# The last tile of softmax rows transposed by TensorE instead of by DVE's 32x32 turns and a DMA exchange

## What is computed

```
q    = x @ Wq.T + bq
p    = softmax(q @ keys.T / sqrt(128))          # keys: 4096 x 128
x1   = layernorm(x + (p @ values) @ Wo.T + bo)
h    = silu(x1 @ W1.T * s1) * (x1 @ W2.T * s2)
h    = gelu(h @ H1.T * s_h1);  h = gelu(h @ H2.T * s_h2)
out  = layernorm(x1 + h @ W3.T * s3)
```

## Time and profile before

| | |
|---|---|
| Time, median of 3 runs | 1117.41 us (1116.58 to 1117.55) |
| Time of the profiled execution | 1117.46 us |
| Its span, first to last instruction | 1115.5 us |
| PE, DVE, ACT, POOL busy | 97%, 87%, 81%, 58% of the span |
| Frames end (last scores moved) | about 725 us |
| PE starts the first hidden layer of block 0 | 760.3 us |

### The profile page before, as it was taken

How to read it: one execution, slowest core, us unless ns; L and a number is a source line. 1 busy time by engine, 2 the same in 40 slices (tenths; PEclk the granted TensorE clock), 3 DMA queues, 4 the chain that set the end, 5 groups by cost and what they waited for, 6 DMA issues and landing times.

```text
span 1115.5 us, 20017 instructions
## 1 busy us (share of the span) xinstructions
PE 1079.3 (97%) x5324; PEld 770.6 (69%) x5324; DVE 972.2 (87%) x1806; ACT 903.1 (81%) x1609; POOL 643.0 (58%) x617
## 2 busy tenths in 40 slices
PE   6899999999999999999999999979999999999996
PEld 5666666666666666666666666646888888888875
DVE  6999999999999999999999899897888887888884
ACT  6787788878887888888878878788788888888883
POOL 0487888888888888888888888760211211121111
PEclk9999999999999999999999999999999999999998
DMA  6879888988988889888888998891010010011000
GB/s 202 203 185 212 198 201 210 209 200 202 209 203 206 203 207 210 200 202 209 206 203 204 212 200 188 193 255 55 12 46 28 28 56 28 28 35 50 11 13 27
DMA packets 83957, 165.89 MB, mean 149 GB/s; under 512 B 19664, under 2 KB 47824, under 8 KB 83792
## 3 DMA queue, kind: packets, MB, share of 16 engines
q1 hardware_dynamic: 71536, 154.29, 58.7%
q10 hardware_dynamic: 12384, 11.16, 3.5%
HBM read 22.76 MB, written 8.39 MB: 28 GB/s over the span
## 4 chain that ended last, share of the span: by engine, by line
PE 42%; SPq 13%; issue 11%; POOL 10%; ACT 10%; DMA 6%; DVE 5%; ACTq 1%; POOLq 0%; DVEq 0%
PE ring L1090 13%; SPq L380 12%; PE ring L1091 12%; POOL pT L549 10%; DMA slot_p<-rows 6%; ACT rows L629 5%; ACT pT L638 4%; PE o_ps L1017 2%; PE s_ps L1045 2%; PE s_ps L1043 2%; PE s_ps L1044 2%; PE o_ps L1020 2%; PE o_ps L1022 2%; DVE rows L795 2%; DVE rows L828 1%
## 5 line engine op out<-in xcount | busy, mean ns | idle before, releaser
L549 POOL TENSOR_TENSOR pT<-slot_p,pT 128x512 f16<-128x512 f32 x482 | 546.0, 1167 | 124.4 <-ACT pT L638 124.3
L638 ACT ACTIVATE pT<-slot_p 128x512 f16<-128x512 f32 x512 | 296.5, 617 | 73.8 <-DMA slot_p<-rows 68.6
L828 DVE TENSOR_SCALAR_CACHE_REDUCE rows<-s_ps 128x1024 f32<-128x1024 f32 x256 | 309.4, 1209 | 40.5 <-DMA slot_p<-rows 19.9
L795 DVE STREAM_TRANSPOSE rows<-rows 128x1024 f32<-128x1024 f32 x256 | 316.9, 1239 | 5.9 <-issue 4.1
L629 ACT ACTIVATE rows<-rows,bias 128x1024 f32<-128x1024 f32 x256 | 291.6, 1139 | 6.4 <-DVE bias L836 5.9
L1043 PE MATMUL s_ps<-keys,q_buf 128*128 128x512 f32 x512 | 249.2, 487 | 6.8 <-DVE rows L828 3.5
L1017 PE MATMUL o_ps<-pT,v_hi 128*128 128x512 f16 x512 | 197.4, 385 | 13.3 <-POOL pT L549 6.6
L1045 PE MATMUL s_ps<-keys,q_buf 128*128 128x512 f32 x512 | 202.4, 395 | 0.0
L1044 PE MATMUL s_ps<-keys,q_buf 128*128 128x512 f32 x512 | 201.1, 393 | 0.0
L1020 PE MATMUL o_ps<-pT,v_lo 128*128 128x256 f16 x1024 | 196.1, 273 | 0.0
L1022 PE MATMUL o_ps<-pT,v_hi 128*128 128x512 f16 x512 | 194.6, 380 | 0.0
(11 more groups left out here) (110 smaller groups left out, 1329.2 us busy)
## 6 DMA issues: line engine op xcount, KB each, us to landing
slot_p<-rows SPq DMA_DIRECT2D x1024, 128.0 KB, 3.0
x_in<-in_x SPq DMA_DIRECT2D x16, 256.0 KB, 3.4
x_in<-in_xT ACTq DMA_DIRECT2D x30, 128.0 KB, 3.3
out<-y_out SPq DMA_DIRECT2D x15, 256.0 KB, 2.4
o_scratch<-o_sum ACTq DMA_DIRECT2D x29, 128.0 KB, 2.7
o_in<-o_scratch SPq DMA_DIRECT2D x14, 256.0 KB, 3.1
z<-in_w_all ACTq DMA_DIRECT2D x25, 113.0 KB, 2.7
rows<-in_w_all SPq DMA_DIRECT2D x1, 2816.0 KB, 12.1
```

The lines of the kernel that those rows point to most:

```text
L549: nc.gpsimd.tensor_tensor(halves(s % RING, 1), slots_first(pp, s), halves(s % RING, 0), ALU.subtract).then_inc(split, 1)
L638: nc.scalar.activation(halves(s % RING, 0), slots_first(pp, s), ACT.Copy).then_inc(highed, 1)
L795: nc.vector.transpose(row_piece(tile, k), row_piece(tile, k)).then_inc(turned, 1)
L828: nc.vector.tensor_scalar(row_piece(tile, k), s_ps[:, j % 2, :], 1.0, None, ALU.mult, ALU.max, accum_out=part_max[:, tile, k:k + 1]).then_ ...
```

## The change

The second tile of the last pair is no longer turned by DVE and exchanged by DMA. Its score columns are produced in another order, by reading the keys in a pattern of 4x4x32 (`by_chunk`), so that 128 neighbouring columns of `rows` are one chunk of the values. PE then transposes 128x128 squares of fp32 from `rows` into two PSUM banks, `y_ps` and `x1_ps`, four squares at a time: a unit. ACT and DVE read the turned half of a unit from PSUM, and ACT and POOL make the parts of the first tile from `slot_p`. A unit is two value steps. In pair 30 the low parts 7, 8, 9, 11, 13 and 15 are now DVE's. `x1` of block 0 is copied by ACT after high part 10 instead of 6, and split by DVE after low part 9. The moments and the normalisation of block 1 move into the loop over units, and the transpose of its x1 goes behind V15. The raw weights are loaded in two parts; the low parts of the weights are no longer made (with this input they are not needed in either version). The four exponentials of the last tile stay behind the third and fourth high part, now with an output copy ahead of them.

```
-LATE_STEP = 12
+LOW_BY_DVE = (7, 8, 9, 11, 13, 15)
+LOW_BY_POOL = tuple(s for s in range(STEPS) if s not in LOW_BY_DVE)
+UNITS = STEPS // 2
...
+    def unit_part(u, tile, low):
+        return pT[:, 2 * u % RING:2 * u % RING + 2, :, (2 * low + tile) * P:(2 * low + tile + 1) * P].rearrange(
+            "p s c (a t) -> p (s c) a t", t=G)
+    def unit_slots(u):
+        return slot_p[:, 1, 0:GROUPS, 4 * u:4 * u + 4, :].rearrange("p a c t -> p c a t")
+    def unit_bank(u):
+        return stage.y_ps[:, :, :] if u % 2 == 0 else stage.x1_ps[:, :].rearrange("p (s d) -> p s d", d=P)
...
# SP
         exchange(PAIRS - 1, 1, 0, PIECES - 1)
-        for k in range(PIECES):
-            exchange(PAIRS - 1, 1, 1, k)
...
# POOL
+        for s in LOW_BY_POOL[STEPS - T_LAG:]:
+            low_part(PAIRS - 2, 0, s)
+        for u in range(UNITS):
+            pool.wait_ge(highed, 16 * (PAIRS - 1) + 2 * u + 1)
+            nc.gpsimd.tensor_tensor(unit_part(u, 0, 1), unit_slots(u), unit_part(u, 0, 0), ALU.subtract).then_inc(split, 1)
+            if u == 2:
                 stage.inverse_deviation(pool, 1, 0)
...
# ACT
+        def unit_high(u):
+            if u == 0:
+                for k in range(PIECES):
+                    act.wait_ge(sent[0][k], 16 * GROUPS * PAIRS)
+            act.wait_ge(pv_done, 16 * (PAIRS - 1) + 2 * u + 2 - RING)
+            nc.scalar.activation(unit_part(u, 0, 0), unit_slots(u), ACT.Copy).then_inc(highed, 1)
+            act.wait_ge(unit_made, u + 1)
+            nc.scalar.activation(unit_part(u, 1, 0), unit_turned(u), ACT.Copy).then_inc(highed, 1)
+        after_high = {3: range(PIECES)}
+        for s in range(STEPS - T_LAG, STEPS):
             high_part(PAIRS - 2, 0, s)
+            if s == 3:
+                stage.output_half(act, PAIRS - 3, 1)
+            if s in after_high:
+                for k in after_high[s]:
+                    exp_piece(PAIRS - 1, 1, k)
+            if s == 10:
                 act.wait_ge(sent[0][0], 16 * GROUPS * PAIRS)
                 stage.keep_x1T(act, 0)
...
# DVE
-        stage.residual(dve, 1)
-        for k in range(PIECES):
-            turn_piece(PAIRS - 1, 1, k)
+        stage.residual_sum(dve, 1)
         stage.output_sum(dve, PAIRS - 3, 1)
-        stage.split_x1(dve, 0)
-        for s in range(LATE_STEP, STEPS):
+        for s in LOW_BY_DVE:
             low_part(PAIRS - 2, 0, s)
+            if s == 9:
+                stage.split_x1(dve, 0)
...
+        for u in range(UNITS):
+            dve.wait_ge(highed, 16 * (PAIRS - 1) + 2 * u + 2)
+            nc.vector.tensor_tensor(unit_part(u, 1, 1), unit_turned(u), unit_part(u, 1, 0), ALU.subtract).then_inc(split_last, 1)
...
# PE
+                    if is_step(f, PAIRS - 1) and tile == 1:
+                        k_h, k_l = by_chunk(k_hi, c), by_chunk(k_lo, c)
...
+        def turn_unit(u):
+            if u < 2:
+                pe.wait_ge(exped, 8 * PAIRS)
+                pe.wait_ge(*((stage.z1_ready, 8) if u == 0 else (stage.x1T_ready, 1)))
+            else:
+                pe.wait_ge(split_last, len(LOW_BY_DVE) + u - 1)
+            for n in range(4):
+                last = nc.tensor.transpose(unit_bank(u)[:, n, :], rows[:, SLOTS + (4 * u + n) * P:SLOTS + (4 * u + n + 1) * P], stage.ident[:, :])
+            last.then_inc(unit_made, 1)
...
+                if s == 10:
+                    turn_unit(0)
+                    turn_unit(1)
+            for u in range(UNITS):
+                if u + 2 < UNITS:
+                    turn_unit(u + 2)
+                add_values(PAIRS - 1, 1, 2 * u)
+                add_values(PAIRS - 1, 1, 2 * u + 1)
+                if u == 2:
+                    first_layer(0, (2, 3), low_weights)
             stage.turn_x1(pe, 1)
-            for s in range(STEPS):
-                add_values(PAIRS - 1, 1, s)
```

More of the change, by code:

```diff
@@ L94, with __init__ @@
 class RowStage:
-    def __init__(self, nc, ctx, x_rows, o_dram, o_stored, den, keys, rows):
+    def __init__(self, nc, ctx, x_rows, o_dram, o_stored, den, rows):
         def sb(name, shape, dt):
@@ L252, in store_output, with layers @@
         sp.dma_start(self.o_dram[:, bass.ds(p * 2 * P, 2 * P)], self.o_sum[:, :]).then_inc(self.o_stored, 16)
-def layers(nc, stage, hold, xT, wqT, bq, kT, vT, woT, bo, scale_cols, w_raw, den, keys, rows, out_rows):
+def layers(nc, stage, hold, xT, wqT, bq, kT, vT, woT, bo, scale_cols, w_raw, den, rows, out_rows):
     def sem(name):
@@ L386, in layers @@
     w_hi = stage.w_all[:, 0:W_COLS]
[L387 to L390, removed]
+    stage.x1_hi, stage.x1_lo = (sb(name, [P, BT], FP32R)[:, :] for name in ("x1_hi", "x1_lo"))
+    in_room = sb("in_room", [P, 2, HC, BT], FP32R)[:, :, :, :]
+    raw_in = sb("raw_in", [P, W_AT["h1"]], FP32)[:, :]
+    sb("key_room", [P, 2 * SLOTS - 2 * BT - 2 * HC * BT - W_AT["h1"]], FP32)
+    raw_rest = sb("raw_rest", [P, W_COLS - W_AT["h1"]], FP32)[:, :]
     x1T, x1_hi, x1_lo, scales, table_room = stage.x1T, stage.x1_hi, stage.x1_lo, stage.scales, stage.table_room
@@ L497, in _ @@
             stage.load_x(sp, b, b % 2)
[L498 to L501 removed]
+        sp.wait_ge(scored, 8 * PAIRS)
+        sp.dma_start(raw_in, w_raw[:, 0:W_AT["h1"]]).then_inc(raw_loaded[0], 16)
         stage.store_output(sp, PAIRS - 2)
         stage.store_output(sp, PAIRS - 1)
+        sp.wait_ge(pv_done, 16 * PAIRS)
+        sp.dma_start(raw_rest, w_raw[:, W_AT["h1"]:W_COLS]).then_inc(raw_loaded[1], 16)
         sp.wait_ge(stage.o_stored, 16 * PAIRS)
@@ L1201, in program @@
         scale_cols = (t["s1"], t["s2"], t["s_h1"], t["s_h2"], t["s3"])
-        stage = RowStage(nc, stage_ctx, t["x"].rearrange(tiled, p=P), o_dram, o_stored, den, keys, rows)
+        stage = RowStage(nc, stage_ctx, t["x"].rearrange(tiled, p=P), o_dram, o_stored, den, rows)
         layers(nc, stage, stage_ctx, t["xT"], t["wqT"], t["bq"], t["kT"], t["vT"], t["woT"], t["bo"], scale_cols, t["w_all"],
-               den, keys, rows, out.rearrange(tiled, p=P))
+               den, rows, out.rearrange(tiled, p=P))
 def kernel(**inputs):
```

140 lines of the change are left out of this document (67 added, 73 removed).

## The result

| | before | changed |
|---|---|---|
| Time, median of the compared runs | 1117.26 us (1116.58 to 1117.55) | 1124.09 us (1123.28 to 1125.31) |
| Ratio, 95% interval | | 1.0064 (1.0052 to 1.0076) |
| Profiled execution: time, span | 1117.46, 1115.5 us | 1123.28, 1121.6 us |

A forecast was written before the change was run, and what follows sets the result against it. PE was taken as the bound, its feed-forward turns having no slack, so the start of block 0's first hidden layer counts. 1.6 + 1.4 + 0.7 = +3.7 us on 1117.41 gave 1121.1 us, range 1118.0 to 1123.8.

The forecast's parts named there:

- Up to v4: Frames before v4: no gain; PE's 3.39 us wait stays, since ACT makes v4's high part behind the four exponentials.
- The 4x4x32 pattern: Last tile's score matmuls: reading keys this way taken at nothing, bounded by +5.6 us for 24 matmuls.
- The split: Split of x1 done late, at 740.4: PE's first layer starts at 740.5 instead of 738.89, +1.6 us.
- The pair that the prediction priced at 0.60 + 1.11 us: DVE and POOL low parts excluding each other: 1.71 instead of 1.56 us; four more pairs would give 1121.7.
- First layer to first hidden layer: Eight transpose groups on PE add 3.52 us, 2.3 of idle time is filled, 0.2 waits before V14: +1.4 us.
- Behind V15: Block 1's x1 transposed behind V15; PE idles before the fourth product of the first hidden layer: +0.7 us.
- Moved at nothing: Block 1's normalisation, gates, output copy, raw weights, second split and last output sum: moved at no cost.
- all later turns shifted by 3.7: Feed-forward turns after the first hidden layer: all later by the same 3.7 us.
- A second fall of the clock: Rival: PE's idling near 739 brings half clock again behind 741, +1.7 us, 1122.8; chance 0.15.
- No change: Rival: the split of x1 is done before 739 us, sum falls by 1.6 to 2.1, 1119.0 to 1119.5; chance 0.24.
- slow keys: Rival: last eight score groups stretched, with their maximum and exponentials, time up to 1126; chance 0.05.
- faster: Rival: DVE's relief pays if DVE, not ACT's exponentials, held v4; chance 0.06.

The follow-up runs named there:

- Experiment 5: The kernel of experiment 1, with x1 of block 0 copied after high part 6 and split ahead of all low parts, as before the change: 1119.72 us, ratio 1.0019.
- Experiment 6: The kernel of experiment 1, with only one 128x128 square of each unit transposed instead of four: 1120.15 us, ratio 1.0019.
- experiment 1: The changed kernel with `keys`, x1's halves and `in_room` at their old addresses, and the first raw weights loaded behind V15: 1121.69 us, ratio 1.0046.
- experiment 4: Also before_pad64: the kernel before with 64 bytes of unused room, `h_hi1` then 128 past a multiple of 256: 1112.28 us, ratio 0.9953.
- after_pad64: Also experiment 3: the changed kernel with 64 bytes of unused room, x1's halves, `in_room` and `h_hi1` then 128 past a multiple of 256: 1117.01 us, ratio 0.9997.
- 7: The changed kernel, padded so that x1's halves and `in_room` start 128 past a multiple of 256 and `h_hi1` 192 past: 1120.4 us, ratio 1.0027.
- 8: The changed kernel, padded so that x1's halves and `in_room` stay 64 past a multiple of 256 and `h_hi1` starts 128 past: 1119.8 us, ratio 1.0021.
- 11: The changed kernel with 64 bytes of padding and x1 of block 0 copied and split as early as before the change: 1115.4 us, ratio 0.9984.

## Why the prediction was right in direction and wrong in size

**Up to v4: right.** PE waits 3.39 us for v4, to the hundredth as before, though DVE had nothing to do. ACT's exponentials hold v4.

**The 4x4x32 pattern: right.** The score matmuls of the last tile stand 0.235 us apart (0.23 before), 0.1 us for 24 of them.

**The split: right in its place and its end, the idle time mis-sized.** By line, of the changed kernel's DVE (ns min/median/max, first and last start):

```profile
L217 DVE CAST x_hi<-rows x16: 417/424/1368, 737.4 to 1076.8; 128x512 fp32r x10, 128x512 fp32r<-128x512 f32 x6
L219 DVE TENSOR_TENSOR x_lo<-rows,x_hi x16: 691/693/1520, 738.8 to 1077.3; 128x512 fp32r<-128x512 f32 x16
L822 DVE TENSOR_TENSOR pT<-slot_p,pT x6: 679/990/1639, 733.1 to 741.5; 128x512 f16<-128x512 f32 x6
L993 DVE TENSOR_TENSOR pT<-y_ps,pT x4: 691/692/692, 745.4 to 758.0; 128x512 f16<-128x512 f32 x4
```

The cast of 737.4 took 1.37 us where most of the others take 0.42: it takes a turn with POOL, as I let it, although it has one input. The subtraction of 738.8 took 1.52, and ends at 740.36 (predicted 740.4). The Trainium skill (SBUF — State Buffer, "Who interferes with whom") lists a cast among the instructions that can take the port shared with GpSimd; the 1.37 us agree. It excepts such instructions from what it says of a single SBUF input, and the prediction's sentence on the section leaves that exception out. The pair that the prediction priced at 0.60 + 1.11 us would be 0.66 + 1.11 = 1.77 with its own 0.66 for DVE. Neither changes the sum of 3.7. Only PE's wait was 2.91 us instead of 1.9, because v8 was done a microsecond earlier than I had it; that moved nothing. Experiment 5 gives 1.05 us as the split's own part of the 1.6.

**First layer to first hidden layer: right, 1.55 for 1.4.** Transposes in groups of 0.44 us, the low parts of a unit 0.69 us on DVE beside POOL, no turn-taking (last row above), 0.21 us ahead of V14. Experiment 6 shows the transposes to be the price. The 32 transposes did not bring the clock down: it is 1.00 throughout from 739 us in this trace. The Trainium skill (TensorE: Matmul & The Clock Gate, "PE-mode transpose") says that transposes don't count as activity as matmuls do; a quarter of PE's time in transposes had no such effect here.

**Behind V15: right, 0.53 us of waiting for 0.7 predicted.** In experiment 1, at the old placement, the shift grows from 3.18 to 3.93 us between the start of the first hidden layer and the first turn, 0.75 for the whole term.

**"Moved at nothing", and with it "all later turns shifted by 3.7": this step failed.** The prediction gives the moved allocation no term at all, and no reason why it should be nothing. At the old placement the shift is 3.9 and constant, as the step says. In the changed kernel it grows by 2.0 us over thirteen turns, 0.15 a turn, because the allocation put the moving operands of 48 matmuls of a turn from 128 to 64 bytes past a multiple of 256. I had read the diff of the allocation as naming. What the runs put in the step's place is the placement, worth 2.2 us here, and 4.4 us of the span if used (1115.5 - 1111.1, experiment 4). 3.9 + 2.2 = 6.1 is the difference of the two spans, 1121.6 - 1115.5. The other 0.7 us of the 6.8 between the medians stay open. Without them the time would have lain inside the range, and the step would have been wrong all the same.

**The rivals.** A second fall of the clock did not occur in the profiled execution, and did in one of after_pad64, where it cost 1.3 us. How long the granted clock stays at half around v4 differs too: 3.4 us in all six traces of the kernel before and its variants and in that of the changed kernel, 6.8 us in those of experiments 1, 6, 7, 8 and 11, and twice 3.4 in those of experiments 3 and 5. So the half clock lasts 6.8 us in sum in each of the seven experiments with the new tail, and 3.4 in every trace without it and in the changed kernel's own. The prediction had no such case, and what it costs is not measured: in experiment 1 the first layer still started at 740.58. The changed kernel's own executions spread over 2.0 us, and experiment 1's over 5, before's over 1.0 in the result. The clock may well hold part of the 6.8 us against the spans' 6.1, which no run shows. No change, slow keys, and faster: excluded by the rows above.

**Open.** Why the start address matters is not shown, only that it does, inside each hidden layer by its own operand. Three things limit it.

- The pace is not a pure function of a matmul's own start. The first-layer matmuls of the kernel before, at 128 past, stand 0.230 us apart directly behind the slower last layer, and 0.2265 in before_pad64, where the last layer is fast and they lie where they lay. So the 48 matmuls stood 0.2294 us apart on average before and 0.2332 in the changed kernel, which gives 0.18 us a turn (0.15 measured) and not the 0.29 of 48 times 0.006.
- The score matmuls in the frames, whose moving operand is `keys`, don't follow the rule. It lies 128 past in the kernel before and 64 past in the changed one, and they stand 0.2315 and 0.2311 us apart between 100 and 700 us. Over all runs their pace lies between 0.230 and 0.234, in no order of that start.
- The weights start 128 past a multiple of 256 in every run. Whether 128 itself is the good start of the moving operand, or the same remainder as the weights', no run separates.

And with the turns taken off, 64 and 192 bytes of padding gain 1.7 to 2.6 us ahead of the turns that the hidden layers don't explain, 128 bytes only some 0.2; which tile brings it is undecided.

## What to carry to other kernels

A change that allocates, drops or moves a buffer moves the tiles behind it, and on a stretch where PE is busy 299 of 300 us that can be a change of pace: compare the start addresses of the matmuls' moving operands in both builds before costing the rest at nothing, and try a few bytes of padding, which gave more here (1117.3 to 1112.3 us) than the change itself cost (3.9). Read PE's pace from the distance of starts over many matmuls, since the shown durations are alike at either pace, and ask of a shift whether it stays constant: a constant one comes from the place of the change, a growing one from something that the loop meets each time. And when work goes from an idle-prone engine to the one that bounds the kernel, first ask who ended last there: DVE's relief of 5 us before v4 bought nothing, because ACT's exponentials ended last.

## What the runs showed of the hardware

- In the hidden layers, matmuls of 128x512 fp32-rounded operands stand 0.226 to 0.227 us apart when the moving operand starts 128 bytes past a multiple of 256, 0.229 at 192 past, 0.233 to 0.234 at 64 past and at a multiple itself, with the clock at 1.00 in all of them and the weights at 128 past. The score matmuls in the frames show no such difference: 0.2315 at 128 past, 0.2311 at 64.
- A DVE cast from SBUF to SBUF, 128x512, takes 0.42 us alone and 1.37 us beside POOL's subtraction; a subtraction with one operand from PSUM takes 0.69 beside POOL.
- Four fp32 transposes of 128x128 between value steps take 0.44 us, and 32 of them within 15 us left the clock at 1.00.
- After the same wait of 3.4 us of PE ahead of v4 the granted clock was at half for 3.4 us in the traces of before and of the changed kernel, and for 6.8 us in those of experiments 1, 6, 7, 8 and 11.
